# Spread of a row from its mean and sum of exponentials in step 0, exponentials issued at other places, and projections reordered, in a two-layer graph kernel

## What is computed

```python
h = jnp.maximum(_layernorm(x, axis=-1), 0.0)
x = x + _L0_gnn_ref(h, adj, ...)          # 4-bit quantised: adj @ relu(quant(h) @ quant(W))
h = jnp.maximum(_layernorm(x, axis=-1), 0.0)
# _L1_gnn_ref(X=h, S=adj):
S = S + jnp.eye(n); R = S / jnp.clip(S.sum(axis=1, keepdims=True), 1e-12)
Xf, Xa = (X, X)
for s in range(2):
    logits = (Xa @ W1) @ W2 @ (Xa @ W3).T
    # rows sorted descending; keep the first k_i = sum(cumsum(softmax) < 0.9) + 1, softmax over the kept
    A = _adj_from_feats(Xa, W1, W2, W3)
    Xf = R @ Xf
    Xa = A @ Xa
    Z = Z + (Xf @ U1s[s] + Xa @ U2s[s])
Y = X + Z                                  # layernorm of Y times gamma plus beta, added to x
```

## Time and profile before

| | |
|---|---|
| median of 3 runs | 1416.79 us (1416.27 to 1417.39) |
| the profiled execution's own time | 1413.95 us |
| its span (first to last instruction) | 1412.2 us |
| granted TensorE clock, mean | 0.942 of 2.4 GHz |
| TensorE matmuls busy | 1211.1 us (86%) |
| VectorE busy | 1091.7 us (77%) |
| ScalarE busy | 613.0 us (43%) |
| GpSimd busy | 273.7 us (19%) |

### The profile page before, as it was taken

How to read it: one execution, slowest core, us unless ns; L and a number is a source line. 1 busy time by engine, 2 the same in 40 slices (tenths; PEclk the granted TensorE clock), 3 DMA queues, 4 the chain that set the end, 5 groups by cost and what they waited for, 6 DMA issues and landing times.

```text
span 1412.2 us, 17981 instructions
## 1 busy us (share of the span) xinstructions
PE 1211.1 (86%) x6042; PEld 589.8 (42%) x6042; DVE 1091.7 (77%) x1863; ACT 613.0 (43%) x1164; POOL 273.7 (19%) x236
## 2 busy tenths in 40 slices
PE   0669999989797998999997998879899679999692
PEld 0224555543243454454453553334444334454351
DVE  7997777714999599799899102899379999999868
ACT  1634554537422564564442336540374254241130
POOL 7033332220422031031121001311001011111011
PEclk9989999998999999999998999999999889999896
DMA  7045665521344001001002003344312201512165
GB/s 238 39 166 197 206 219 188 173 105 49 104 135 134 1 31 62 14 31 47 30 30 75 6 25 119 112 175 152 106 30 82 83 16 53 162 40 68 52 228 175
DMA packets 56310, 139.73 MB, mean 99 GB/s; under 512 B 9568, under 2 KB 9568, under 8 KB 52128
## 3 DMA queue, kind: packets, MB, share of 16 engines
q1 hardware_dynamic: 56224, 138.71, 29.2%
HBM read 88.62 MB, written 50.07 MB: 98 GB/s over the span
## 4 chain that ended last, share of the span: by engine, by line
PE 42%; DVE 28%; issue 12%; ACT 9%; DMA 4%; POOL 3%; SPq 1%; DVEq 1%; POOLq 0%; ACTq 0%
DVE WS L1430 10%; PE UB L701 6%; PE RB L863 3%; PE AB L863 3%; PE AB L691 3%; PE AB L684 3%; PE XB L701 3%; ACT E L1118 3%; PE RB L701 3%; DVE w L1644 3%; PE RB L808 2%; PE TB L710 2%; POOL RT L591 2%; DMA AD<-xu_d 2%; PE AB L808 2%
## 5 line engine op out<-in xcount | busy, mean ns | idle before, releaser
L1430 DVE SCALAR_TENSOR_TENSOR WS<-E,g 128x2048 bf16<-128x2048 f32 x128 | 315.1, 2512 | 28.2 <-ACT E L1118 27.1
L1513 DVE TENSOR_REDUCE g<-E 128x1 f32<-128x2048 f32 x32 | 73.0, 2281 | 113.1 <-ACT E L1091 112.9
L1160 ACT ACTIVATE turns<-TB 128x512 f16<-128x512 f32 x128 | 75.7, 594 | 148.9 <-PE TB L716 148.7
L710 PE MATMUL TB<-ident,E 128*128 128x128 f32 x512 | 83.7, 293 | 41.2 <-DVEq L1704 29.3
L591 POOL TENSOR_TENSOR RT<-RT,AD 128x512 f32<-128x512 f32 x32 | 54.0, 1688 | 293.7 <-ACT RT L1130 293.6
L710 PEld LDWEIGHTS TB<-ident,E 128*128 128x128 f32 x512 | 67.5, 151 | 67.4 <-DVEq L1704 31.7
L1154 ACT ACTIVATE turns<-TB 128x512 f16<-128x512 f32 x128 | 75.6, 594 | 39.0 <-PE TB L710 38.9
L1607 DVE SCALAR_TENSOR_TENSOR E<-E,g 128x2048 f32<-128x2048 f32 x33 | 80.2, 2461 | 12.8 <-issue 12.6
L1091 ACT ACTIVATE E<-LB 128x512 f32<-128x512 f32 x128 | 75.5, 598 | 22.2 <-PE LB L783 20.5
L606 POOL TENSOR_TENSOR XHL<-WF,XHL 128x512 f16<-128x512 f32 x16 | 25.6, 1601 | 292.9 <-ACT XHL L1175 292.9
L716 PE MATMUL TB<-turns,minus_e 128*128 128x512 f16 x128 | 52.0, 410 | 33.4 <-ACT turns L1154 33.4
(11 more groups left out here) (309 smaller groups left out, 2428.8 us busy)
## 6 DMA issues: line engine op xcount, KB each, us to landing
turns<-adj_parts SPq DMA_DIRECT2D x48, 512.0 KB, 3.8
E<-adjT SPq DMA_DIRECT2D x16, 1024.0 KB, 7.6
adj_parts<-turns SPq DMA_DIRECT2D x16, 1024.0 KB, 5.2
AH<-adj_parts SPq DMA_DIRECT2D x16, 512.0 KB, 3.8
z_d<-UO SPq DMA_DIRECT2D x31, 256.0 KB, 2.3
XR<-x SPq DMA_DIRECT2D x4, 1024.0 KB, 11.9
WS<-U SPq DMA_DIRECT2D x4, 1024.0 KB, 6.1
x_d<-E SPq DMA_DIRECT2D x16, 256.0 KB, 2.0
```

The source lines that it names most:

```text
L710: i = mm(bank[:, k * P:(k + 1) * P], src(k), ident32[:, :], is_transpose=True, start=(k == 0), stop=(k == KC - 1), skip_group_check=True)
L1160: a(ET[:, 1, c * KC:(c + 1) * KC, :].rearrange("p b c -> p (b c)"), TB[c % 2][:, :], ACT.Copy, scale=SE).then_inc(s_et, 1)
L1430: return v.scalar_tensor_tensor(junk[t % 2], e, g4[:, k, t:t + 1], e, op, ALU.mult, accum_out=g4[:, F_, t:t + 1])
```

## The change

It does seven things. (1) Step 0 has no squares: the variance is computed as 2 (ln(mean of exponentials) - (mean - maximum)), from the sum of exponentials, after the wait for them. (2) Guess constants of step 0 are other ones (1.3 for 1.2816, overshoot 1.3 for 1.2). (3) `early(g)` takes the place of EARLY: all four exponentials (and maxima) of group 1 stand in `group_start` of group 0, and two of groups 2 and 3 as before. (4) The other two of groups 2 and 3 are issued one by one at two earlier places of tile 0. (5) The last tile of layer 0 makes its query and key projection before the two large ones. (6) So does the last tile of step 0. (7) GpSimd and ScalarE take these in the same new order.

```diff
-Z_P, PHI_P = 1.2816, 0.1755
+Z_P, PHI_P = (1.3, 1.2816), 0.1755
-OVERSHOOT = (1.2, 1.2)
+OVERSHOOT = (1.3, 1.2)
-EARLY = 2
+def early(g):
+    return G if g <= 1 else G // 2
...
-            v_lo(T - 1, of(VR, T - 1))
-            pk_lo(T - 1, 0, T - 1, s_vl, T)
+            pk_lo(T - 1, 0, T - 1, s_vl, T - 1)
+            v_lo(T - 1, of(VR, T - 1))
...
-            def post(t):
+            def post(t, last=False):
+                if last:
+                    pk_lo(t + T, 1, t, s_wl, t - OPEN)
                 q.tensor_tensor(XHL[:, 1, :], WF[:, :], XHL[:, 0, :], ALU.subtract).then_inc(s_wl, 1)
-                pk_lo(t + T, 1, t, s_wl, t + 1 - OPEN)
+                if not last:
+                    pk_lo(t + T, 1, t, s_wl, t + 1 - OPEN)
...
+            def post0_last(n):
+                pe.wait_ge(s_xTc, n + 1)
+                pk_product(n, XB)
+                pe.wait_ge(s_ue, n + OPEN)
+                three(UB[:, :], xh, xl, lambda k: U10p[:, k, 0, :], lambda k: U10p[:, k, 1, :]).then_inc(s_u, 1)
+                pe.wait_ge(s_ve, n + OPEN)
+                three(RB[:, :], xh, xl, lambda k: U11p[:, k, 0, :], lambda k: U11p[:, k, 1, :]).then_inc(s_v, 1)
...
             def last_post():
-                x_turned(2 * T - 1)
-                x_rest(2 * T - 1)
+                n = 2 * T - 1
+                x_turned(n)
+                x_rest(n)
+                pe.wait_ge(s_ue, n + OPEN)
+                pe.wait_ge(s_pkc, n + OPEN)
+                pe.wait_ge(s_xTc, n + 1)
+                pk_product(n, UB)
+                w_product(T - 1)
+                pe.wait_ge(s_pkc, n + 1 + OPEN)
                 u_product(T - 1)
-                w_product(T - 1)
-                p_and_k(T - 1)
...
-            def post0(t, more=True):
+            def post0(t, last=False):
+                if last:
+                    pk(t, 0, t, XB)
                 act.wait_ge(s_u, t + 1)
...
-                pk(t, 0, t, XB)
+                if not last:
+                    pk(t, 0, t, XB)
...
-                for t in range(G):
-                    squared(gq * G + t, (gq % 2) * G + t)
+                if s:
+                    for t in range(G):
+                        squared(gq * G + t, (gq % 2) * G + t)
...
                 for t in tiles:
-                    act.wait_ge(s_sq, 2 * qq + 2 + OPEN)
+                    if s:
+                        act.wait_ge(s_sq, 2 * (qq - T) + 2 + OPEN)
...
             def tile(s, g, i):
+                split = i == 0 and g < NG - 1 and early(g + 1) < G
...
                 if more:
                     e_hi(qq + 1, 0)
+                if split:
+                    terms(s, g + 1, range(G // 2, G // 2 + 1))
                 if post:
                     xT_lo(t - 1 + T)
                     post_out(t - 1)
                 if more:
                     e_lo(qq + 1, 0)
                     e_hi(qq + 1, 1)
+                if split:
+                    terms(s, g + 1, range(G // 2 + 1, G))
                 if post:
                     w_out(t - 1)
                 if ahead:
                     logits_out(qq + 2 * G, slot, (2, 3))
-                    squared(qq + 2 * G, slot)
-                if i == 0 and g < NG - 1:
-                    terms(s, g + 1, range(EARLY, G))
+                    if s:
+                        squared(qq + 2 * G, slot)
...
                 if s + g == 0:
-                    terms(s, 1, range(EARLY))
+                    terms(s, 1)
...
                 if s == 0:
                     dve.wait_ge(s_exp, G * gq + G)
-                    ct(v.scalar_tensor_tensor(row(LNU), tot[:, sl].bitcast(I32), 2.0, row(LNU), ALU.mult, ALU.add))
-                    ct(v.tensor_scalar(row(U).bitcast(I32), row(LNU), UNIT - FLOOR * PER_E, UNIT - CAP[s] * PER_E,
-                                       ALU.max, ALU.min))
+                    ct(v.tensor_scalar(row(LNU), tot[:, sl].bitcast(I32), 2.0 / PER_E,
+                                       -2.0 * (UNIT + LOG_N * 2.0 ** 23 - SKEW) / PER_E, ALU.mult, ALU.add))
+                    ct(v.scalar_tensor_tensor(row(VAR), row(MEAN), -2.0, row(LNU), ALU.mult, ALU.add))
+                    ct.free(v.tensor_tensor(row(LNU), row(LNU), row(MEAN), ALU.subtract))
+                    spread(ct, 1e-6)
+                    ct(v.scalar_tensor_tensor(row(A1), row(SIG), -Z_P[0] / 2, row(LNU), ALU.mult, ALU.add))
+                    ct(v.tensor_scalar(row(A1), row(A1), -FLOOR, -CAP[s], ALU.max, ALU.min))
+                    ct(v.tensor_scalar(row(U).bitcast(I32), row(A1), PER_E, UNIT, ALU.mult, ALU.add))
...
                     if g == 0:
-                        largest(g, gq, ct, slice(0, EARLY))
-                    largest(g, gq, ct, slice(EARLY, None))
+                        largest(g, gq, ct, slice(0, G))
+                    elif early(g) < G:
+                        largest(g, gq, ct, slice(early(g), G))
...
                     if g < NG - 1:
-                        largest(g + 1, gq + 1, ct, slice(0, EARLY))
+                        largest(g + 1, gq + 1, ct, slice(0, early(g + 1)))
```

More of the change, by code:

```diff
@@ L1057, in post0 @@
                 a(UO[:, :], UB[:, :], ACT.Copy, scale=SV / (SX * SW)).then_inc(s_ue, 1)
-                if more:
+                if not last:
                     x_hi(t + 1)
@@ L1235, in group_start @@
                     if g < NG - 1:
-                        terms(s, g + 1, range(EARLY))
+                        terms(s, g + 1, range(early(g + 1)))
                     pk(t - 1 + T, 1, t - 1, UB)
```

50 lines of the change are left out of this document (26 added, 24 removed).

## The result

The changed kernel takes 1375.91 us (median of 4 runs, 1374.86 to 1379.57) against 1417.09 (median of 4, 1416.27 to 1419.2) of the kernel before: ratio 0.9712, 95% interval 0.969 to 0.9734. The forecast was 1376.0 in a range of 1369 to 1387. Executions of the kernel before differ by more than these four show: beside the later runs it took 1408.0 to 1419.1, so the 41.2 us between the medians is partly a matter of which executions were met.

The account below looks back on a forecast made before the run. No single engine was taken to bound the kernel: the chain runs over all, with TensorE and VectorE waiting in turn. Terms summed to -40.4 us, giving 1373.6 us profiled and 1376 us median, range 1369 to 1387.

Parts of the forecast that it names:

- -7.2: Start of step 0: without the idle gap and at the upper clock, TensorE starts the R products 7.2 us earlier.
- The clock rival: First logits stages of both steps: the clock stays low, gain only 35.0 us, 1382 us; chance 0.17.
- Term (c): Start of step 0: without squares, R product 2's 3.72 us low-half wait and 1.5 us of slow clock go, -5.2.
- The +4.0: Head of group 0, step 0: four exponentials ahead of the first high half give back 4.0 of TensorE's 12.4 us.
- the 12 us of idle time: Sign at the head of group 0, step 0: TensorE's idle time there grows to some 12 us.
- The first pass of group 1 near 449: Sign in step 0: VectorE's search of group 1 starts near 449 instead of 477.67.
- -16.8: Step 0: group 2 starts 16.8 us earlier, with VectorE setting its start.
- -17.0: Step 0: group 3 starts 17.0 us earlier, the 8.06 us wait in front of it staying.
- -4.1: End of step 0 and step 1's first logits: less idle time and the upper clock save 4.1 us.
- -19.3: Step 1: VectorE's 19.26 us wait in its third pass goes, and the end follows VectorE, 19.3 us earlier.
- The slower rival: Search in step 0: a row misses the new guess, its tile takes 42 passes, 99 us and more, 1475; chance 0.01.

Follow-up runs that it names:

- The last run: Changed kernel with three search rounds and other constants in step 0, first chunks of tiles 1 to 3 waiting only for their bank's copy: 1365.24 us.
- The runs with two and two: Changed kernel with group 1's exponentials two ahead of group 0 and two in its tile 0: both steps 1388.4 us, step 0 only 1379.54 us.

## Why the prediction was right

**Order of the tails.** Right in mechanism and nearly in sum (-7.6 from L733 for -7.2), by two errors that cancelled. The first chunk came earlier by more than the 3.0 forecast: 12.54 us from L733 before, 7.59 now, -5.0, because the clock was 0.66 in 304 to 309 of the trace before and is 1.00 now, which the prediction had not looked at. That is in part luck: all four traces with the old order take 12.5 to 12.7 us there, but of the ten with the new order five show the lower level behind L733 and take 1.5 to 1.7 us more than the 7.59. The logits stage was sized at 2.85 us a tile from the second stage and takes 3.43. The step that failed is that transfer: in the second stage a tile's first chunk waits only for the copy that frees its bank, in the first for all four copies of the tile before. The last run takes that wait away and gets 2.86. The clock rival (low in both stages) did not come; the clock is 1.00 with TensorE 57 to 69% busy. The Trainium skill, "TensorE: Matmul & The Clock Gate", Part 1, says that activity releases the throttle; the trace agrees in so far as a stage with waits of 0.35 to 1.06 us kept the upper level, while the one behind 3.27 us of idle time ran at the lower for most of its length before and for some 4 us in the run with both old tails.

**The low half and the squares.** Term (c), -5.2, was right in mechanism (the wait is gone, and putting the squares back brings it back). From the first R product to the end of the last one ahead of group 0 it is 114.1 us before and 108.5 now, -5.6, and where the wait returns it costs 3.77 + 2.66 = 6.4.

**Four exponentials ahead of group 0.** The +4.0 measures 2.4, and the 12 us of idle time that the text named as a sign are 10.4: 1.65 in front of the masked tile and 8.74 behind it, for 8.03. The two more exponentials do take 4.0 us of ScalarE. But ScalarE had waited 2.87 us before them for GpSimd's sum of an R row, and waits 1.45 now: that sum fell beside two passes of VectorE before and falls into VectorE's 3.00 us of idle time now. GpSimd's timeline, before and changed:

```profile
447.63 2.68 POOL L591 TENSOR_TENSOR RT<-RT,AD 128x512 f32<-128x512 f32 x1 [7.12 <-ACT RT L1130]
```

```profile
436.56 1.26 POOL L595 TENSOR_TENSOR RT<-RT,AD 128x512 f32<-128x512 f32 x1 [7.09 <-ACT RT L1155]
```

The runs with two and two have 2.59 and 2.63 us there again. So counted from L733 TensorE resumes 10.9 us earlier, not 8.4; that the table shows 8.5 is the 2.4 us of its first line and no merit of the forecast.

**Groups.** The first pass of group 1 near 449 came at 448.63, group 2 at -17.1 for -16.8. Group 3 came at -16.2 for -17.0, with a wait of 9.13 where 8 was said. Counted from L733 these are -19.5 and -18.6, so both were forecast somewhat too small. That group 1's order in step 0 pays is what the traces of the two runs with two and two show; the prediction had charged it only as a cost of 4.0, and had not said that VectorE would be late for group 1 otherwise.

**End of step 0.** -4.1 was forecast; from the start of group 3 to the R products of step 1 it is 100.95 us before and 96.37 now, -4.6. The first logits chunk came at 843.14 for the 843 named.

**Step 1.** -19.3 was forecast; from the start of its R products to the end it is 537.1 before and 518.8 after: -18.3. The wait of 19.26 is gone. TensorE's 9.19 became 2.67 and 2.07 in two waits, for 4 to 6 in one. At group 3 2 us were lost against the forecast, on VectorE's side: TensorE waits 12.44 us there, as it did before (12.56).

**The slower rival.** Its mechanism is real and it was held for nearly impossible: 0.01. On these inputs the changed kernel does not meet it; but if the row of the float32 working is the one that bisects, 5 values stand against a limit of 6 on the low side, a margin of one and not of the three that the text's 5 and 8 suggest, and taking the constant back by 0.02 costs 185 us. The price was also too low: 99 us and more, from 42 passes of 2.35, where a round takes 4.07 and the count of equals adds 21.

## What to carry to other kernels

A wait that several engines share in turn is best found by its place in the order: issuing two exponentials of group 1 earlier in step 1 was worth 19 us, and the removal of 32 squares 7 at most. Before a pace is carried over from one stage to another, compare the wait conditions of the two stages, not only the instructions. And a guess whose miss falls back on a slow path is a cliff: work out how far the worst row is from it, take as the limit what a run that fell back shows, and price the whole fallback, with the small instructions around its passes.
